# One transformer stack on one core: a head's keys by three loads of 48, 32 and 16 rows instead of six of 16, queries likewise, and a value projection moved beside a chain of norms

## The reference, cut to what matters

```python
# L0_xattn: keys and values from the context, then from a side input of 256 rows
# L1_xattn: keys and values from the context
score = jnp.einsum('bhqd,bhkd->bhqk', qh, kh) * scale   # 16 heads of 16, B = 2
attn = jax.nn.softmax(score, axis=-1)
out = jnp.einsum('bhqk,bhkd->bhqd', attn, vh)
```

```python
qn = q / jnp.maximum(jnp.linalg.norm(q, axis=-1, keepdims=True), 1e-12) * safe_scale
q_hyp = _expmap0(qn)     # k alike; v takes no part in this
```

## Time and profile before

| | us |
|---|---|
| median of 3 runs | 2609.09 (2606.3 to 2609.96) |
| the profiled execution, its own time | 2608.86 |
| its span in the trace | 2607.0 |
| L0 context attention, first maxima to last | 71 to 518 |
| L1 context attention, first maxima to last | 1012 to 1411 |
| PE busy | 2349.4 (90%) |
| DVE busy | 1474.7 (57%) |
| ACT busy | 1070.1 (41%) |
| DMA queue of SP and ACT, share of 16 engines | 30.9% |

### The profile page before, as it was taken

The page is one execution under the profiler, slowest core; times in us unless marked ns, Lnnn a source line. Parts: engine busy times, 40 slices in busy tenths (PEclk is TensorE's granted clock), DMA queues, the critical chain, the costliest instruction groups (busy, mean ns, idle before and its releaser), DMA issues. The chain is left out here.

```text
span 2607.0 us, 39087 instructions
## 1 busy us (share of the span) xinstructions
PE 2349.4 (90%) x15277; PEld 1361.9 (52%) x15277; DVE 1474.7 (57%) x2363; ACT 1070.1 (41%) x1957; POOL 381.0 (15%) x659
## 2 busy tenths in 40 slices
PE   3899999988999998999999687888989999898789
PEld 1344444435599663445444444352238657565447
DVE  4777777723222456888885586236877433323444
ACT  2466666623111233777777374134332233121320
POOL 2454000001000400000000161002630000000100
PEclk8799999998899997999999868998898999989799
DMA  7887454211544498655541101001006340100200
GB/s 202 233 193 172 86 113 76 33 55 47 234 193 195 145 275 247 134 96 94 126 68 19 48 1 62 30 1 67 0 32 223 117 170 1 61 1 1 106 1 9
DMA packets 108358, 258.61 MB, mean 99 GB/s; under 512 B 11824, under 2 KB 83088, under 8 KB 94096
## 3 DMA queue, kind: packets, MB, share of 16 engines
q1 hardware_dynamic: 104144, 213.73, 30.9%
q0 software_dynamic: 2736, 39.37, 4.5%
q10 hardware_dynamic: 1296, 3.03, 0.3%
HBM read 211.26 MB, written 44.83 MB: 98 GB/s over the span
## 5 line engine op out<-in xcount | busy, mean ns | idle before, releaser
L815 DVE TENSOR_REDUCE sta_parts<-sta_psA 128x1 f32<-128x1024 f32 x544 | 625.8, 1187 | 186.9 <-PE sta_psA L730 185.2
L873 ACT ACTIVATE sta_probs<-sta_psS 128x512 f32<-128x512 f32 x1056 | 575.9, 597 | 273.9 <-PE sta_psS L741 271.7
L741 PE MATMUL sta_psS<-L_xattn_qS,L_xattn_kst 99*128 99x256 bf16 x2112 | 356.0, 278 | 11.4 <-ACT sta_probs L873 6.6
L730 PE MATMUL sta_psA<-L_xattn_kst,L_xattn_qS 99*128 99x512 bf16 x1088 | 293.3, 387 | 46.3 <-PEq L59 31.4
L741 PEld LDWEIGHTS sta_psS<-L_xattn_qS,L_xattn_kst 99*128 99x128 bf16 x2112 | 161.4, 98 | 258.7 <-ACT sta_probs L873 183.2
L750 PE MATMUL sta_psO<-sta_probs,L_xattna_V 128*32 128x256 f32 x2560 | 189.5, 385 | 0.0
L730 PEld LDWEIGHTS sta_psA<-L_xattn_kst,L_xattn_qS 99*128 99x128 bf16 x1088 | 104.3, 99 | 131.0 <-DVE sta_parts L815 43.8
L1160 ACT ACTIVATE sht_probs<-sht_psS 128x768 f32<-128x768 f32 (+1 forms) x64 | 55.3, 863 | 151.5 <-PE sht_psS L1001 99.1
L590 POOL CAST sta_split<-sta_neg 128x2 bf16<-128x2 f32 x64 | 12.1, 188 | 714.7 <-issue 466.5
L750 PE MATMUL sta_psO<-sta_probs,L_xattn_V 128*32 128x256 f32 x1536 | 114.4, 389 | 0.0
L750 PEld LDWEIGHTS sta_psO<-sta_probs,L_xattna_V 128*32 128x32 f32 x2560 | 82.5, 109 | 51.4 <-issue 20.9
(11 more groups left out here) (611 smaller groups left out, 4001.9 us busy)
## 6 DMA issues: line engine op xcount, KB each, us to landing
L_xattn_kst<-L_xattn_keys SPq DMA_DIRECT2D x186, 136.0 KB, 5.1
L_xattn_kst<-L_xattn_keys SPq DMA_DIRECT2D x186, 128.0 KB, 4.7
L_xattn_values<-prj_rows SPq DMA_DIRECT2D x64, 256.0 KB, 3.9
L_xattn_keys<-prj_parts SPq DMA_DIRECT2D x32, 384.0 KB, 4.1
L_xattna_V<-in_ctxV SPq DMA_DIRECT2D x5, 2048.0 KB, 12.0
L_xattna_V<-L_xattn_values SPq DMA_DIRECT2D x5, 2048.0 KB, 11.1
l2f_W<-in_M SPq DMA_DIRECT2D x10, 1024.0 KB, 8.4
L_xattn_keys<-sta_bparts SPq DMA_DIRECT2D x24, 384.0 KB, 6.9
```

The source lines that it names most:

```text
L730: last = nc.tensor.matmul(psA[:, u % 2, col:col + rhs.shape[1]], lhsT, rhs, start=True, stop=True)
L741: last = nc.tensor.matmul(psS[:, at % 2, j * T:(j + 1) * T], lhsT, rhs, start=True, stop=True)
L815: nc.vector.tensor_reduce(into(parts[:, u // n % 2]), view(psA[:, u % 2, :]), AX.X, ALU.max).then_inc(max_taken, 1)
L873: nc.scalar.activation(probs[:, u % NP, i * 512:(i + 1) * 512], psS[:, at % 2, :], ACT.Exp, scale=scale).then_inc(probs_ready, 1)
```

## The change

`key_pieces` yields three loads in place of six: parts 0 to 2 into 48 rows, parts 0 and 1 into 32, part 0 into 16. The source of the first is `scratch[0:3, 16 rows, cols]`, which counts 3, then 16, then the columns; its destination counts 48 rows. `stack_pieces` still yields six loads, now one for each half of the heads and each group of 48, 32 and 16 rows, whose source repeats one part three times, twice or once. In `hyperbolic_attention` the value projection leaves the first `gemms` stage; PE makes it in the stage of norms, followed by 24 products that nobody reads, and DVE adds the bias in four pieces (`add_bias_to`).

```diff
 def key_pieces(dst, scratch, h, cols):
-    return [(dst[i * D:(i + 1) * D, cols], scratch[part, h * D:(h + 1) * D, cols]) for i, part in enumerate(K_PARTS)]
+    out, at = [], 0
+    for n in (3, 2, 1):
+        out.append((dst[at:at + n * D, cols], scratch[0:n, h * D:(h + 1) * D, cols]))
+        at += n * D
+    return out
...
-def stack_pieces(dst, scratch, parts):
-
-    return [(dst[i * D:(i + 1) * D].rearrange("d (m h) n -> d m (h n)", m=KC), scratch[part].rearrange("(m d h) n -> d m (h n)", m=KC, d=D))
-            for i, part in enumerate(parts)]
+def stack_pieces(dst, scratch):
+    out, at = [], 0
+    for part, n in ((0, 3), (1, 2), (2, 1)):
+        src = scratch[part].rearrange("(m d h) n -> d m (h n)", m=KC, d=D)
+        for m in range(KC):
+            rows = dst[at:at + n * D].rearrange("p (m h) n -> p m (h n)", m=KC)[:, m, :]
+            out.append((rows, src[:, m, :].unsqueeze(0).to_broadcast([n, D, 8 * NTOK])))
+        at += n * D
+    return out
...
-                                 "s", bias=w["bgates"], ones=ones)
-                  + project_rows(w["v"], 512, xnT, lambda t: vadd(nc, v[:, t, :], w["bv"]), "v"),
+                                 "s", bias=w["bgates"], ones=ones),
...
+                @block.tensor
+                def _(pe):
+                    for t in range(NT):
+                        for k in range(KC):
+                            last = nc.tensor.matmul(values[:, t, :], xnT[:, k, t * P:(t + 1) * P], w["v"][:, k, :], start=k == 0, stop=k == KC - 1)
+                        last.then_inc(value_product, 1)
+                    for _ in range(PAUSE):
+                        nc.tensor.matmul(unread[:], K["ident16"], K["mask16_q"], start=True, stop=True)
...
+                    def add_bias_to(t):
+                        dve.wait_ge(value_product, t + 1)
+                        step(V.tensor_tensor(v[:, t, :], values[:, t, :], w["bv"], ALU.add))
...
+                    add_bias_to(0)
                     dve.wait_ge(squares_ready, 1)
...
+                    add_bias_to(1)
                     dve.wait_ge(norms_ready, 1)
...
+                    for t in range(2, NT):
+                        add_bias_to(t)
```

More of the change, by code:

```diff
@@ L1422, in value_loads @@
             return [(V[g % 3][:], scrv[g // 4, g % 4])]
-        query_loads = stack_pieces(qS, scrq, Q_PARTS)
+        query_loads = stack_pieces(qS[0:STACK], scrq)
         key_ones = [lambda engine, i=i: engine.memset(kst[i][SHIFT:], 1.0) for i in range(4)]
@@ L1891, in hyperbolic_attention @@
     NQ = 2 * H
+    PAUSE = 24
     NAMES = ("qE", "kE", "qH", "kH")
@@ L1936, in hyperbolic_attention @@
             first = sq[:].rearrange("p t h d -> p (t h) d")[:, :, 0]
-            with stage(nc, "dve_step", "squares_ready", "sums_ready", "norms_ready", "times_in", "times_ready", "om_ready", "plain_ready") as \
-                    (block, dve_step, squares_ready, sums_ready, norms_ready, times_in, times_ready, om_ready, plain_ready):
+            with nc.psum_tensor("l1b_values", [P, NT, 512], F32) as values, nc.psum_tensor("l1b_unread", [P, 512], F32) as unread, \
+                    stage(nc, "dve_step", "squares_ready", "sums_ready", "norms_ready", "times_in", "times_ready", "om_ready", "plain_ready",
+                          "value_product") as \
+                    (block, dve_step, squares_ready, sums_ready, norms_ready, times_in, times_ready, om_ready, plain_ready, value_product):
+                @block.tensor
[6 more added lines that the diff above has]
+                        nc.tensor.matmul(unread[:], K["ident16"], K["mask16_q"], start=True, stop=True)
                 @block.gpsimd
```

## The result

The changed kernel takes 2709.36 us (median of 4 runs, 2707.02 to 2714.21) beside 2609.39: 1.040 times the time before, with a 95% interval of 1.0375 to 1.0416. The forecast was 2650. The direction and the cause came out as forecast; the size did not: +98.0 us between the two spans (2607.0 and 2705.0) where +41 was forecast, and L1, which was forecast as just covered, lost almost as much as L0.

What follows compares the result with a forecast made beforehand. PE paces the two context attentions by head, with loads covered, not by much in L0. Confined key loads: 42 (L0) + 10 (L1) - 3 - 3 (openings) - 5 (L1_attn) = +41 on 2608.9, 2650 us; range 2612 to 2716.

Steps and rivals of the forecast that it cites:

- just covered: L1 context attention: 12.3 us of loads against 12.52 a head, so only the start is lost, 10 us.
- Then two engines carry 16 + 16 + 1 = 33 rows of each head: Key loads split by first count: two engines carry 33 rows a head, a third 17, thirteen carry one.
- The rival of 16 engines: Key loads spread over 16 engines by rows, keys stay covered: 2598 us, between 2580 and 2608; chance 0.16.
- every row at 1.13 us: Rival for key loads: 37 us a head, some 25 more for 62 heads, 4100 us; chance 0.02.
- With three engines in place of 16 at work it is far nearer the first; I take 0.36 in L0 and 0.34 for L1's 8192 bytes: Key row's cost on a lone engine, bounds 0.31 and 1.13 us; gives 11.9 and 11.2 us a head.
- The prediction's bounds: Dear side of the row price: L0 loses 66 us at 0.40 a row, L1 41 at 0.376.
- L1's period unchanged: Sign of being right: L1's time per head stays, 12.52 us before.
- a period above 12.5: Sign of being wrong: L1's period above 12.5 us throughout, standing for the crowded case.
- the crowded case: Rival: the key loads' 3 engines get in each other's way; about 2825 us, chance 0.10.
- The rival of three engines in each other's way: Two of three engines share one way for a 48-row load, 5.0 us more a head: about 2825; chance 0.10.
- Openings: Starts of L0 and L1, where query and key loads from POOL's queue are fewer: -3 us each.
- L1_attn: Value projection moved to the norms: first stage -9.3 us, DVE's additions give part back; -5 in all.

Runs made afterwards that it cites:

- run 2: Changed kernel with the 16 rows as outermost count in key and query loads, parts inside: 2586.39 us, ratio 0.9938 to the kernel before.
- run 13: Changed kernel where SP waits for head 1's keys to land before issuing the first value load and all that follows: 2713.65 us.
- Run 3: Changed kernel with only one row of 128 loaded from the fourth value load on: 2675.97 us.
- run 9: Changed kernel with each pair of L0's context fetches issued one head earlier: 2709.01 us.
- runs 8 and 12: Run 8: changed kernel with 16 outermost in the 48-row load (and queries' group of 48) alone, 2645.96 us; run 12: also context fetches a head earlier, 2630.68 us.
- Run 4: Changed kernel with the groups reversed to 16, 32, 48 rows, so the 48-row load writes partitions 48 to 95: 2707.03 us.
- run 6: Kernel before with the L1_attn edit (the diff of hyperbolic_attention) alone: 2596.93 us, ratio 0.9964.
- run 10: Changed kernel with each context attention's first value load issued after the keys of heads 1 and 2, not between them: 2719.06 us.

## Why the prediction was right in its mechanism, and the step that failed

**Right: where the rows go.** "Then two engines carry 16 + 16 + 1 = 33 rows of each head" is what the slices of L1 show, and run 2 turns it off with nothing changed but the order of the counts. The rival of 16 engines is out. So is "every row at 1.13 us".

**The step that failed: "With three engines in place of 16 at work it is far nearer the first; I take 0.36 in L0 and 0.34 for L1's 8192 bytes".** The mechanism held, and the price did for a row by itself: 0.33 us in L0 (run 13), 26 GB/s in both stages. The premise didn't hold. Three engines are not at work alone; value loads and fetches run on the other 13 at the same time. Spread over the rows, with the forecast's other terms kept, the periods give: L0's first 14 heads took (339.46 - 80.5) / 14 = 18.5 us each where 16.9 was forecast, which is (18.5 - 5.0) / 33 = 0.41 us a row. L1 took 13.7 a head where 12.3 was forecast: (13.7 - 1.1) / 33 = 0.38. In L1 this mattered most, since 12.3 and 13.7 lie on either side of the head's 12.52.

```profile
339.46 0.16 DVE L832 TENSOR_REDUCE sta_neg<-sta_parts 128x2 f32<-128x10 f32 x1
```

The prediction's bounds come close at these prices, 66 us for L0 at 0.40 (64.1 measured) and 41 for L1 at 0.376 (46.8 measured), but in L1 that is in part luck. The bound had 14 us at the start and 1.0 for each later head. The trace has 25 at the start, since the first three heads took 63.1 us where they took 38.0 before, and then 21 in five heads, each behind a value load; the heads between keep their 12.3 to 12.8. So the prediction's sign "L1's period unchanged" did not come, and its sign of being wrong, a period above 12.5, came for one head in four, without the crowded case that it stood for.

```profile
1091.23 0.16 DVE L832 TENSOR_REDUCE sta_neg<-sta_parts 128x2 f32<-128x8 f32 x1
...
1154.32 0.16 DVE L832 TENSOR_REDUCE sta_neg<-sta_parts 128x2 f32<-128x8 f32 x1
```

**Why a row was dearer.** A lone engine does move its rows at 26 GB/s, but not beside a value load: the engines together then give 232 GB/s, half of what 16 in step give. I had priced the value load on the loaded engines at 4.6 us, its time when nothing runs beside it. An estimate of what it cost there: four heads are 132 rows, at 26 GB/s 41.6 us, and four late heads of L1 took 54.64, which leaves 13.0. Run 3 shows the same in the stage: without five value loads L1 is 20.9 us shorter. At a stage's start, run 13 puts 6 of the 9 us that keys 1 were late beyond the forecast on the loads beside them.

**What I hadn't seen: the path through POOL.** I counted only keys as late. The fetches pass through the same engines, POOL waits for them in order, and PE waits for POOL, 37.0 us against 14.9. It did not change the sum at 33 rows (run 9), but at 20 rows it is most of L0's loss (runs 8 and 12).

**What I hadn't priced: the clock.** 24.7 us of the 111 in L0 and L1 are the same products taking longer, at a mean clock of 0.91 and 0.92 for 0.97. Idle time cost more than a quarter above its own length (24.7 on the 86.4 us that were added, 29%).

**The rival of three engines in each other's way** (2825) asked for 5.0 us more a head from one shared way to the buffers. Run 4, which moves the three to other partitions, is the same within 3 us, and late in L1 three engines move 26 GB/s each, so it doesn't pace the stage. Something of it is there all the same, in the first keys of run 13 (59 GB/s for 78), where the keys were 3 us later by themselves than forecast. That it fades fits the prediction's own argument against it, that the third engine runs ahead and is then out of step, but no run tests this.

**Openings: -1.6 and +5.8 for -3 and -3.** With the queries' halves alone (run 1) the first head's maxima in L0 were reduced at 86.9 (one trace each), with the keys' three loads alone (run 5) at 87.9, with both at 80.5, with neither at 82.1 and in run 6 at 81.3. The two edits don't add up, and why is open. With 16 outermost it is 76.3, and the stretch between the two attentions 500.0 for 504.9: there the fewer, wider loads gain 10.7 us in the two openings.

**L1_attn: -4.0 for -5.** As forecast but for the clock. The last gates start at 1574.2, the first addition 3.8 us later, and after 4.5 us of idle the transposes start at the lower clock and stay there longer than before (3.15 for 2.38 in their second group):

```profile
1593.23 3.65 PE L390 MATMUL gem_banks<-top_consts_weights,l1b_R_qE 128*128 128x128 f32 x16 [4.54 <-PEq L59]
...
1596.66 3.15 PE L390 MATMUL gem_banks<-top_consts_weights,l1b_R_kE 128*128 128x128 f32 x16
```

**The other 13.1 us behind L1** lie in stages that no edit touches. They were not forecast, and they hide that much of the miss. The same stretch of layer 3, first of before, then of the changed kernel:

```profile
2290.00:2370.00 80.00, 72.55 (x635) 53.86 (x633) 20.57 (x39) 20.76 (x35) 5.23 (x24) 0.88 0.00 1
```
```profile
2394.00:2470.00 76.00, 68.53 (x630) 51.45 (x626) 19.26 (x36) 21.51 (x34) 5.23 (x24) 0.91 0.01 1
```

4 us less, all of them PE's busy time, at a granted clock of 0.91 for 0.88. Such stretches came out in one of two lengths, some 2 to 4 us apart, in trace after trace, whatever the kernel. From the first `hyp_D` (1495.31 before) to the end, every one of the other fifteen traces is shorter than the one of before, by 3.2 to 13.4 us. What sets the length is open, and a term of a few us can't be read from the difference of two spans here.

**Sum.** 64.1 + 46.8 - 1.6 + 5.8 - 4.0 - 13.1 = 98.0. Against the forecast's 41, L0 is 22 more, L1 37, the openings 10 and L1_attn 1, and the 13.1 take some of it back.

## What to carry to other kernels

When loads are merged to save issues, look first at the outermost count of both sides: with the count that 16 divides outside, three loads did a little better than six here; with the 3 outside they cost 100 us. When a transfer falls on few engines, price it with its neighbours, the loads that run on the other engines meanwhile too, since everything whose rows pass those engines is late with it, and follow each of them to the in-order engine that waits. For a stall of the tensor engine add the products that run at the lower clock behind it; where a forecast stands near the point at which a period tips from hidden to bound, give the dear side of the bound its weight.

## What the runs showed of the hardware that was not expected

- Merging with 16 outermost made the key loads faster, not only fewer: 168 to 236 GB/s into 48 and 32 partitions where most slices into 16 had 113 to 128, and a DMA share of 0.72 for 0.86 over the same four heads' window.
- Two or three engines on keys and the others on a value load moved 232 GB/s together at 101% busy. Before, the value load alone moved 453 to 463.
- A value load issued behind two heads' keys still ran beside the first: engines that the keys don't use go on to what stands next in the queue (run 10).
- Three engines on one head's keys moved 59 GB/s at its start and 78 late in L1, as busy each time (18.9% and 18.6% of 16).
- SP itself stood where loads had piled up: three key issues took 2.00 us at 69.36 and 11.11 at 95.35 in the changed kernel:

```profile
69.36 2.00 SPq L695 DMA_DIRECT2D L_xattn_kst<-L_xattn_keys  x3
...
95.35 11.11 SPq L695 DMA_DIRECT2D L_xattn_kst<-L_xattn_keys  x3
```
